# One kernel of attention and experts: slot rows made by TensorE, more operands kept on chip, longer weight ring, shorter tile pipeline

## What is computed

```python
x = layernorm(x + attention(x))     # 32 heads of 64, decayed linear attention, RMS norm, sigmoid gate
x = layernorm(x + experts(x))

# experts(x): 64 experts of 256 -> 96 -> 256, 6 per token, capacity 48
scores = sigmoid(x @ gate_w)
topk_w, topk_ids = grouped_topk(scores + bias)              # 4 of 8 groups, then 6 experts
buf[e, slot] = x[token]                                     # at most 48 tokens per expert
h = silu(buf @ w_gate[e]) * (buf @ w_up[e])
y[token] += topk_w * (h @ w_down[e])
y += silu(x @ ws_gate) * (x @ ws_up) @ ws_down              # shared expert, every token
```

## Time and profile before

| what | us |
|---|---|
| median of 3 runs (1378.43 to 1380.31) | 1379.14 |
| the profiled execution, its own time | 1375.23 |
| its span in the trace | 1373.4 |
| PE busy in the span | 1299.2 (95%) |
| DVE busy | 1168.1 (85%) |
| ACT busy | 956.7 (70%) |
| POOL busy | 439.5 (32%) |

### The profile page before, as it was taken

The page is one execution under the profiler, slowest core; times in us unless marked ns, Lnnn a source line. Parts: engine busy times, 40 slices in busy tenths (PEclk is TensorE's granted clock), DMA queues, the critical chain, the costliest instruction groups (busy, mean ns, idle before and its releaser), DMA issues.

```text
span 1373.4 us, 39715 instructions
## 1 busy us (share of the span) xinstructions
PE 1299.2 (95%) x15212; PEld 1083.1 (79%) x15212; DVE 1168.1 (85%) x2455; ACT 956.7 (70%) x1751; POOL 439.5 (32%) x292
## 2 busy tenths in 40 slices
PE   7999999999999999999999999999999999979850
PEld 5888888888888888888888888888888888865420
DVE  6989989898989898989989898989898999843227
ACT  7777777777777777777777777777777777644325
POOL 0222323332322333232233232322323232434554
PEclk9999999999999999999999999999999999999885
DMA  8500000000001010000000000001000000598958
GB/s 313 210 2 17 27 17 26 17 26 17 26 9 34 2 36 7 17 26 17 26 17 26 17 26 17 26 9 34 2 21 22 17 27 17 175 315 249 258 110 310
DMA packets 52679, 88.14 MB, mean 64 GB/s; under 512 B 5088, under 2 KB 32064, under 8 KB 51648
## 3 DMA queue, kind: packets, MB, share of 16 engines
q1 hardware_dynamic: 42368, 71.62, 15.6%
q0 software_dynamic: 4608, 7.08, 2.7%
q10 hardware_dynamic: 5568, 7.34, 1.5%
HBM read 60.71 MB, written 25.31 MB: 63 GB/s over the span
## 4 chain that ended last, share of the span: by engine, by line
PE 89%; DMA 5%; DVE 2%; issue 2%; ACT 1%; POOL 1%; SPq 0%; ACTq 0%; DVEq 0%; POOLq 0%
PE pA L526 25%; PE pB L526 24%; PE pO L623 12%; PE pC L610 10%; PE pS L588 10%; PE pC L526 2%; DMA sb_stage<-gather_rows,sb_gidx 2%; DMA sums<-sb_stage,sb_sidx 1%; DMA sb_W<-sums 1%; DMA sb_stage<-wprep 1%; PE pS L805 1%; PE pB L787 1%; PE pS L813 1%; PE pS L787 1%; PE pC L645 1%
## 5 line engine op out<-in xcount | busy, mean ns | idle before, releaser
L1540 POOL TENSOR_TENSOR sb_acc<-sb_acc,sb_sq 128x512 f32<-128x512 f32 x112 | 246.2, 2198 | 681.6 <-ACT sb_sq L912 681.6
L526 PE MATMUL pB<-sb_xh,sb_W 128*128 128x256 f16 x2048 | 350.7, 273 | 0.0
L526 PE MATMUL pB<-sb_xl,sb_W 128*128 128x256 f16 x1024 | 279.2, 273 | 0.0
L1149 DVE TENSOR_TENSOR sb_S<-pS,sb_D 128x1024 f32<-128x1024 f32 x250 | 231.6, 949 | 36.2 <-PE pS L588 35.5
L1155 DVE TENSOR_TENSOR sb_Shl<-sb_S,sb_Shl 128x1536 f16<-128x1536 f32 x122 | 220.1, 1804 | 2.4 <-ACT sb_Shl L901 2.4
L526 PEld LDWEIGHTS pB<-sb_xh,sb_W 128*128 128x128 f16 x2048 | 193.0, 99 | 31.6 <-issue 0.2
L901 ACT ACTIVATE sb_Shl<-sb_S 128x1024 f16<-128x1024 f32 x244 | 192.2, 835 | 12.2 <-DVE sb_S L1149 2.3
L526 PE MATMUL pA<-sb_xh,sb_W 128*128 128x256 f16 x1024 | 175.8, 274 | 5.6 <-DVE sb_W L1107 5.6
L526 PE MATMUL pA<-sb_W,sb_xh 128*128 128x256 f16 x1024 | 177.1, 275 | 3.2 <-ACT sb_qh L868 3.1
L623 PE MATMUL pO<-sb_Wo,sb_yh 128*128 128x256 f16 x1024 | 174.7, 273 | 1.5 <-DVE sb_yl L1128 1.5
L1128 DVE TENSOR_TENSOR sb_yl<-sb_y,sb_yh 128x512 f16<-128x512 f32 x128 | 161.5, 1262 | 2.1 <-ACT sb_yh L917 2.1
(11 more groups left out here) (231 smaller groups left out, 2653.8 us busy)
## 6 DMA issues: line engine op xcount, KB each, us to landing
sb_stage<-wprep SPq DMA_DIRECT2D x7, 1280.0 KB, 6.2
sb_W<-sums SPq DMA_DIRECT2D x16, 512.0 KB, 11.9
sb_W<-w_experts SPq DMA_DIRECT2D x16, 384.0 KB
gather_rows<-sb_xr SPq DMA_DIRECT2D x16, 320.0 KB, 2.3
sb_D<-w_experts SPq DMA_DIRECT2D x12, 384.0 KB
sb_xs<-xT SPq DMA_DIRECT2D x17, 256.0 KB, 2.8
sb_D<-decay SPq DMA_DIRECT2D x8, 512.0 KB, 7.4
sb_xn<-x SPq DMA_DIRECT2D x16, 256.0 KB, 2.9
```

The lines of the kernel that those rows point to most:

```text
L526: last = nc.tensor.matmul(dst, a, m, start=(i == 0), stop=(i == len(terms) - 1), **kw)
L1149: nc.vector.tensor_tensor(scores_at(h)[:, :, a:z_], pS[:, :, a:z_], d[:, :, 0:z_ - a], ALU.mult).then_inc(s_Sm, 1)
L1540: nc.gpsimd.tensor_tensor(acc[:, :], acc[:, :], sq[:, :], ALU.add).then_inc(s_acc, 1)
```

## The change

1. **Slot rows by PE.** The transfers of `ids` and their buffers go. PE multiplies a tile's column of numbers, broadcast to 128 columns as the stationary operand, by the identity, which leaves the numbers along each row. The first four tiles are made in `pO` before unit 11; later ones one by one in `merge`, in the free half of `pM`, four tiles ahead. DVE compares one tile per iteration instead of four every fourth iteration. The first four comparisons now stand ahead of the products of units 10 and 11.
2. **Halves of ten sequences kept.** ACT and DVE write the halves of sequences 1 to 10 straight into the old staging buffer, which has room for ten units. They are neither stored nor loaded back. Five units are loaded. The hardware loops of the other engines become two loops (1 to 10, 11 to 15).
3. **Ring of 21 pairs, 16 ahead.** `S` and `Shl` hold one pair each, `W` ten, `D` six, `Wo` three. Pairs 12 to 15 are issued between `store_x1` and `store_rows` of the last sequence. Later pairs wait for the `down` of tile `p - 17`, and the ring's reuse comes at pair 21.
4. **One tile between stages.** On PE an iteration is gate and up of tile `p`, down of `p - 1`, transposition of the rows of `p + 1`, transposition of the inner values of `p`, merging of `p - 1`.

The core of the diff:

```diff
-RING = 16
+RING = 21
-UNIT_EARLY = 3
+KEPT = 10
-FIRST_PAIRS = 12
+FIRST_PAIRS = 16
...
-        xgT = carve(P, KINDS + 1, NC * P).rearrange("p s (c n) -> p s c n", c=NC)
+        xgT = carve(P, 2, NC * P)
+        xgT = [xgT[:, 0, :], xgT[:, 1, :]] + [v32[:, t, :] for t in range(NT)]
...
+        in_w, in_d, in_wo = 10, 6, 3
+        last_two = [a.rearrange("p h n -> p (h n)") for a in (S[:, :, :], whole_S[1])]
...
+        def split_rows(b, kept, part):
+
+            if kept:
+                return xe[:, bass.ds((b - 1) * (2 * NC * T) + part * NC * T, NC * T)]
+            return x1hl[:, part, :, :].rearrange("p c n -> p (c n)")
...
                 store_x1(b)
-                store_split(b)
+                if not kept:
+                    store_split(b)
                 store_rows(b)
...
-            sp.wait_ge(s_x1s, 16 * SEQS)
-            sp.wait_ge(s_wl, parts_split(NQ - 1, PARTS))
-            for j in range(UNIT_EARLY):
+            sp.wait_ge(s_x1s, 16 * (SEQS - KEPT))
+            sp.wait_ge(s_g, STEPS)
+            for j in range(KEPT, SEQS - 1):
                 load_unit(j)
...
+            for p in range(in_w, 12):
+                load_pair(p)
             store_x1(SEQS)
+            for p in range(12, FIRST_PAIRS):
+                load_pair(p)
             store_rows(SEQS)
-
-            sp.wait_ge(s_ids, 1)
-            sp.dma_start(ids_main, ids[:, 0:BLOCK]).then_inc(s_idr, 16)
-            sp.dma_start(ids_rest, ids[:, BLOCK:CAP]).then_inc(s_idr, 16)
-            sp.wait_ge(s_idr, 32)
...
             for p in range(FIRST_PAIRS, PAIRS):
-                sp.wait_ge(s_md, p - FIRST_PAIRS + 1 if p < RING else KINDS * ((p - RING) // 4 + 1))
-                load_pair(p, p % RING)
+                wait(sp, s_md, p - FIRST_PAIRS - 1)
+                if p >= RING:
+                    sp.wait_ge(s_md, KINDS * ((p - RING) // 4 + 1))
+                load_pair(p)
...
+            pe.wait_ge(s_idx, 1)
+            for t in range(EQB):
+                last = nc.tensor.matmul(pO[:, t * P:(t + 1) * P], slotf[:, t:t + 1].broadcast_to([P, P]), ident[:, :], start=True, stop=True)
+            last.then_inc(s_idr, 1)
             for u in "g11 d10 d11".split():
                 unit(u)
...
             def merge(t):
+                pe.wait_ge(s_eq, min(t + EQB, TILES))
+                wait(pe, s_wo, t)
+                if t + EQB < TILES:
+                    spread_ids(t + EQB, pM[:, HID:HID + P])
                 pe.wait_ge(s_ysb, t + 1)
-                pe.wait_ge(s_eq, t + 1)
-                wait(pe, s_wo, t)
                 nc.tensor.matmul(pM[:, 0:HID], equal[t % EQS], ysb[t % 2], start=True, stop=True).then_inc(s_mm, 1)
...
-            for p in range(TILES + 3):
+            for p in range(TILES + 1):
+                if p < TILES:
+                    gate_up(p)
+                if p >= 1:
+                    down(p - 1)
                 if p + 1 < TILES:
                     transpose_tokens(p + 1)
                 if p < TILES:
-                    gate_up(p)
...
+                    transpose_inner(p)
+                if p >= 1:
+                    merge(p - 1)
```

More of the change, by code:

```diff
@@ L341, in block_kernel @@
         s_x1r = sem("s_x1r")
-        s_un = [sem(f"s_un{i}") for i in range(2)]
+        s_un = sem("s_un")
         s_ugu, s_uact, s_ush = sem("s_ugu"), sem("s_uact"), sem("s_ush")
@@ L351, in block_kernel @@
         s_slots = sem("s_slots")
-        s_ring = [sem(f"s_ring{i}") for i in range(RING // 4)]
+        s_ring = [sem(f"s_ring{i}") for i in range(PAIRS // 4)]
         s_gath = [sem(f"s_gath{i}") for i in range(XRING)]
@@ L358, in block_kernel @@
         s_sc = [sem(f"s_sc{i}") for i in range(2)]
-        s_idr, s_idb = sem("s_idr"), [sem(f"s_idb{i}") for i in range(2)]
+        s_idr = sem("s_idr")
         s_eq, s_place, s_sidx = sem("s_eq"), sem("s_place"), sem("s_sidx")
@@ L386, in sequences @@
                 step(0, q)
-            with eng.Fori(1, SEQS) as b:
+            with eng.Fori(1, KEPT + 1) as b:
+                for q in range(NQ):
+                    step(b, q, True)
+            with eng.Fori(KEPT + 1, SEQS) as b:
                 for q in range(NQ):
@@ L489, in _, with load_pair @@
-            for r in range(in_w):
-                load_pair(r, r)
+                sp.dma_start(units[j].rearrange("p w c n -> p (w c n)"), x1_split[j]).then_inc(s_un, 16)
+            def load_pair(p):
+                r = p % RING
+                sp.dma_start(ring[r][:, 0:4 * NC * FF], w_experts[p]).then_inc(s_ring[p // 4], 16)
+                sp.dma_start(ring[r][0:FF, 4 * NC * FF:PAIR_W], w_down[p]).then_inc(s_ring[p // 4], 16)
+            sp.wait_ge(s_x1s, 16 * (SEQS - KEPT))
+            sp.wait_ge(s_g, STEPS)
@@ L1043, in evacuate @@
                 if kind < 2:
-                    last = nc.scalar.activation(xgT[:, kind, :, :], bank, ACT.Copy)
+                    last = nc.scalar.activation(xgT[kind], bank, ACT.Copy)
                 else:
                     for h in range(2):
-                        to, at = [a.rearrange("p c (j h n) -> p c j h n", j=4, h=2)[:, :, :, h, :] for a in (xgT[:, kind + h, :, :], bank)]
+                        to, at = [a.rearrange("p c (j h n) -> p c j h n", j=4, h=2)[:, :, :, h, :] for a in (xgT[kind + h], bank)]
                         last = nc.scalar.activation(to, at, ACT.Copy)
@@ L1073, in _ @@
             evacuate(0)
-            for p in range(TILES + 2):
+            for p in range(TILES + 1):
+                if p < TILES:
+                    inner(p)
+                if p >= 1:
+                    weighted(p - 1)
                 if p + 1 < TILES:
@@ L1465, in find_equals @@
                 nc.vector.tensor_copy(sidx[:, a:z_], placed[:, a:z_]).then_inc(s_sidx, 1)
-            find_equals(0)
+            dve.wait_ge(s_idr, 1)
+            chain.ready()
+            for t in range(EQB):
+                find_equals(t, pO[:, t * P:(t + 1) * P])
+            place_rows(0)
+            for j in (UNITS_AHEAD - 2, UNITS_AHEAD - 1):
+                unit_product(j)
             def evacuate(t):
```

117 lines of the change are left out of this document (48 added, 69 removed).

## The result

The changed kernel takes 1382.63 us (median of 20 runs, 1380.09 to 1387.60), the kernel before, run beside it, 1379.71 (20 runs, 1377.14 to 1382.53): a ratio of 1.0021 with a 95% interval of 1.0012 to 1.003. The forecast was 1372.0, with 1378.5 as the upper end, so the result lies above the whole range. The profiled execution took 1380.36 us with a span of 1378.5.

The account below looks back on a forecast made before the run. PE was taken to bound the kernel from 60 to 1180 us, so only the last 193 us could move. Start -2.4, loop -2.0 and after the last copy -2.8 gave -7.2 us: 1372.0 us, range 1366.5 to 1378.5.

Parts of the forecast that it names:

- Main loop, 0: Main part, 60 to 1180 us: the change's new work lies beside a PE that never waits, costing 0 to +1 us.
- Start, -2.4: Start of the tiles: first gate and up at 1234.1 instead of 1236.5, rows landing at 1227.7; ends -4 and 0.
- Loop, 86.2 us: Tile loop, first gate and up to last copy: 86.2 us instead of 88.2, so -2.0 us.
- the cover just holds: Transposition of inner values: product ready 0.76 us after gate and up, PE filled 0.87 us; uncovered +1.0 and +0.5 us.
- the first 20: Row products made inside the tile loop: 20 at 0.25 us each on PE, +5.0 us; ends 0 and +11.
- Rival 3: PE waits at the inner transposition in each tile; 0.45 us per tile adds 10.8 us, giving 1383; chance 0.06.
- DMA contention, +1.5: Tile loop: weight loads beside gathers and scatters need 3.5 us per tile against PE's 3.4; +1.5 us, ends 0 and 5.
- rival 2: Scatters stay slow, DVE's copies wait for them between tiles 8 and 14: 1378; chance 0.15 with a late start.
- a first gather after 1230: Start of the tiles: listed as a sign that the forecast is wrong; the first gather was expected near 1228.4.
- the three spells of the earlier trace: Tile loop before the change: PE's three slow-clock spells, put at 6.9 us lost against 2.4 GHz.
- After the last copy, 4.4 us from its start: End of the tile loop: last scatter finds a free queue, 4.4 us instead of 7.2, so -2.8 us; ends -3 and 0.
- the hand-overs: After the last copy: 0.2 us for hand-overs, beside 0.42 for the copy and 3.75 for the landing.

Follow-up runs that it names:

- e2: Changed kernel with the old order of the tile loop on PE, ACT and DVE; 11 us under the change's median.
- e4: Changed kernel with the old tile-loop order and pairs 12 to 15 loaded behind the last store of rows; 1368.58 us.
- e5: Changed kernel with the spread product moved from the merge to ahead of the inner product's transposition; 2.95 us slower than e8.
- e8: Changed kernel with pairs 12 to 15 behind the last rows and the spread product ahead of the inner transposition; 1365.3 us, ratio 0.9898.
- e17: Changed kernel without an edit, run beside e18; ratio 1.0009 to the kernel before.
- e18: Same code as e3, run again in a later session beside e17; 1378.64 us, ratio 0.9985 to the kernel before.
- e1: Kernel before with only the tile loop's order changed to one tile between stages; ratio 0.9966 to the kernel before.
- e3: Changed kernel with pairs 12 to 15 issued behind the last store of rows instead of ahead of it; 1365.56 us.
- e6: e3 with the first gather held until pairs 12 to 15 have landed; first gather 7 us later and 4 us slower beside e8.
- e11: Changed kernel with each tile's spread (number-row) product issued twice in the merge; loop 86.9 us, 3.8 us slower beside e12.
- e12: Changed kernel with POOL issuing the scatter of tile p ahead of the gather of tile p + 8; 3.8 us less than e11.
- e9: Changed kernel without an edit, run again beside the kernel before; ratio 1.0018.

## Why the prediction was wrong

**What the runs show, part by part**, each within a session: pairs 12 to 15 ahead of the rows cost 2.91 (e2 to e4), 2.95 (e5 to e8) and 3.14 us (e17 to e18); the short order is worth 6.2 us on the kernel before (e1) and 3.0 on the rest of the change with rows first (e4 to e3), in a session without late signals. These are differences of small sets of runs: each of the 3 us can be off by 2 us or more, and that of e2 and e4 is by itself not clear of zero. The late signals cost 13.1 us (e3 to e18). The kernel before isn't slower where the changed ones have them: its medians are 1379.7 to 1380.2 us in sessions 1, 2 and 4 and 1379.7 to 1380.6 in 0, 3, 5 and 6. It was not profiled in those sessions, so whether it has late signals there is not known.

Between the profiled executions the forecast misses by 1.1 us up to the first gate and up (1235.20, forecast 1234.1), by 10.5 in the loop (96.7, forecast 86.2) and by 0.6 behind it (5.0, forecast 4.4): 12.2 of 12.4 us, and six sevenths of it in the loop.

*Main loop, 0*: right; the 0.6 us of the first 40 us is their usual scatter.

*Start, -2.4*: wrong in the landing of the rows. I netted the units that are no longer loaded against the four pairs and got 0.5 MB, so 8.2 us to the landing. With four pairs ahead ten profiles show 8.8 to 14.2, 11.2 in the mean; with two and with three, 8.3; with none, 3.2 to 5.0, 4.0 in the mean. The difference of none and four, 7 us, is what 2.4 MB take at the 344 GB/s of the earlier trace rows, 6.9 us. What I had wrong is the other side. With no pairs ahead the kernel with all its units lands the rows in 6.7 (before) and 6.2 us (e1), the changed one in 4.0. So seven units less gave some 2.5 us, not the 5.3 of 1.8 MB. More was hardly there to win: in e3 the last of pairs 0 to 11 lands 0.9 us behind the issue of the rows (1220.61, issue 1219.72), and the rows of sequence 15, stored beside an almost idle queue, took 2.3 to 2.7 us in all profiles.

Of the 7 us by which rows first lands them sooner only about 3 reach the kernel's time, because pairs 12 to 15 then load beside the first gather. The first gather's time to landing, in e3 and in e5:
```profile
DMA to landing us min/median/max: 7.4/7.4/7.4
```
```profile
DMA to landing us min/median/max: 4.3/4.3/4.3
```
From the first gather to the first gate and up are 7.9 to 8.7 us with rows first, 5.2 to 6.1 with four pairs ahead, and 5.5 in e6, whose gather waits for the pairs. Also, with rows first the gather waits for its indices, which let it start 7.2 us behind the issue of the rows, however soon these land. With pairs ahead, row products and finds hid under the wait, as said. The first gate and up came 15.1 to 20.7 us after the issue, forecast was 14.6.

*Loop, 86.2 us*: the failing step is "a product ready 0.76 us behind gate and up, a cover of 0.87, so the cover just holds". As arithmetic it was right. In the seven profiles with the short order, the change's other parts and no late signals the product comes as PE gets to the transposition (e3: 2.0 us of standing in all, although in 17 of 24 tiles the transposition starts within 0.1 us of the product's end: no slack is left), the granted clock is at its upper level from tile 2 on, and the loop takes 81.1 to 83.1 us, 86.9 with e11's doubled products; the forecast, to the end of the copy, is 86.6. The doubled products cost 3.8 us beside e12, against the 5.0 at which I had put the first 20. But the step took the 0.06 us from PE's end to ACT's start as a constant, because the one trace showed no other. With late signals that link is 0.35 to 2.0 us in 14 of 48 places of the change, and the short order has no slack for it; the old order has 1.3 to 5.8 us at `transpose_inner`. By the windows above, the 14.6 us between the loops of e3 and e18 are 9.2 us more in which PE stands (11.2 instead of 2.0) and 5.4 us more in which it is busy (84.63 instead of 79.20) with the same matmuls, in longer spells at 1.2 GHz (e18's granted clock is 0.94 over the loop, e3's 0.98). Of the 16.0 us between e3's and the change's, again 5.4 are longer busy time (84.61) and the rest is standing. That the old order would ride out late signals by its slack is inferred from the steady medians of the kernel before; the old order with the change's other parts (e2, e4) was run only without them. Rival 3 named the place and a price, 0.45 us a tile, that is near the measured 12.1 / 24 = 0.50. Its cause, DVE's other work and a cover too short by itself, isn't what happened.

*DMA contention, +1.5, and rival 2*: no copy waited for scatters in the changed kernel; a first gather after 1230 came true in eight of the ten profiles with four pairs ahead, by the landing. On the Trainium skill's rule of turns (DMA: Bandwidth & Descriptors, "Queues, rings and completion order") no run here decides. Two small slips, which change nothing: the three spells of the earlier trace rows add up to 6.8 us, not 6.9, and from pair 18 on the load of pair `p` waits for the `down` of tile `p - 18` (tiles counted from 0), not `p - 17`.

*After the last copy, 4.4 us from its start*: the mechanism was right, the hand-overs too small. From its end it is 4.5 to 4.7 us, so 4.9 to 5.1 from its start, in all sixteen profiles with the short order and the change's other parts, and 6.5 and 6.8 from its end with the old order. The last scatter is issued 0.76 us behind the copy's end (1332.34 to 1333.10), where I had 0.2.

In a session without late signals the change itself was never run. From e3 plus 2.9 to 3.1, and from e2 less 3.0, I estimate 1368.5 us, 0.8% faster than before. With late signals it is slower by 0.2, 0.2 and 0.1% (1.0021, 1.0018, 1.0009; the interval of the third, 0.9998 to 1.002, takes in no change). So the forecast's sign would have been right in one kind of session, by this estimate, and even there its time is 3.5 us too high. The best that was run is rows first in the short order, 1365.3 us with the moved spread product (e8; 0.9898, 0.9882 to 0.9915) and 1365.6 without it (e3), both without late signals; with them it is 1378.64 (e18; 0.9985, 0.9974 to 0.9996). So it is below the kernel before in both kinds of session, and below the change in the one in which both ran. Rows first in the old order (e4, 1368.58) was not run with them. Since the kernel before is not slower with them, e4 may be the safer choice; that is an inference, not a measurement.

## What to carry to other kernels

Slack between engines insures against latencies that the trace at hand doesn't show: take it out only where all that it saves is worth more than a link that turns out 2 us long. A store whose landing others wait for goes ahead of bulk loads in its queue. The bytes that still stand ahead of it when it is issued give its delay, here to within some 3 us; bytes that would have landed by then anyway give nothing back. What moves behind the store then loads beside the transfer that follows, which took back some 3 of the 7 us here. And compare versions only within a session: here one unchanged kernel differs by 13 us between sessions while the reference beside it stays within 1, so that a stable reference doesn't vouch for the comparison.

## What the runs showed of the hardware

The late signals weren't expected. Their release often falls 1.4 to 1.6 us behind the start of a scatter's issue of 1.59 us on POOL (1.53 us at tile 17 of the change, 1.45 in e18), and for gathers 0.8 us behind the start in tile 0 of the change and of e9, whose PE stood at different points then. But in sessions without them signals fall into the same issues and pass in 0.06 us (scatter at 1256.65 of e12, gate and up done at 1257.04). So POOL's issues may set when a held signal goes, not whether signals are held. What makes a session the one or the other stays open: a session is also one chip and one stretch of time, and sessions 2 and 5 report the same chip number.

Whether PE signals late or computes later than its modelled ends say can be told where signals come in bunches. At tile 17 ACT's silu (L1072) waits for gate and up and its weighting (L1089) for the down behind it. In e3 they start at 1292.34 and 1292.77, 0.43 us apart, which is the time that PE takes for the down. In the change they start at 1306.62 and 1306.77, in e18 at 1304.34 and 1304.49: 0.15 us apart. That is too short for a down, so the down had been done by then and its signal was held too. The trace's own times of the signals, which no view prints, say the same: gate and up, down and the next transposition signal at 1306.60, 1306.69 and 1306.73, where PE's records end at 1304.60, 1305.04 and 1305.40; in e3 at 1292.31, 1292.75 and 1293.09. In the eight profiles of the short order without late signals, gate and up and the down behind it never signal less than 0.43 us apart; in each of the nine with them, five or six such pairs are 0.09 us apart. So there PE's signals were held, and released together. Late signals that come singly, as in tile 0 of the change, where gate and up and the transposition behind it were both late by 1.7 to 1.8 us, would fit either. What holds the signals is not shown.
